# Context of batch 0 loaded in the front part of self-attention, its rounding released by the last residual

## The reference

```
x = layernorm(x + self_attention(x))          # 16 heads of 32, causal
x = layernorm(x + cross_attention(x, ctx))    # one head of 512: softmax(q k^T) v
x = layernorm(x + ffn(x))                     # a gated recurrence over the 16 batches
```

## Time and profile before

| | us |
|---|---|
| median of 3 runs | 1415.57 |
| lowest, highest | 1415.21, 1418.94 |
| the profiled execution | 1416.02 |
| its span | 1414.1 |
| self-attention, about | 0 to 381 |
| cross-attention, about | 381 to 837 |

### The profile page before, as it was taken

How to read it: one execution, slowest core, us unless ns; L and a number is a source line. 1 busy time by engine, 2 the same in 40 slices (tenths; PEclk the granted TensorE clock), 3 DMA queues, 4 the chain that set the end, 5 groups by cost and what they waited for, 6 DMA issues and landing times.

```text
span 1414.1 us, 28483 instructions
## 1 busy us (share of the span) xinstructions
PE 1385.4 (98%) x10017; PEld 1211.0 (86%) x10017; DVE 921.9 (65%) x1911; ACT 731.6 (52%) x1989; POOL 569.7 (40%) x475
## 2 busy tenths in 40 slices
PE   7999999999999999999999999999999999999997
PEld 4677777777789999999999988999999999999775
DVE  4589989999657756776677663345453444536697
ACT  4488888888565566656665655222232222222232
POOL 2476767676476565656565620000000000010264
PEclk9999999999999999999999999999999999999999
DMA  7014323335366675667567953010010100000353
GB/s 212 25 56 107 104 75 81 104 104 156 109 172 215 200 240 182 204 195 233 188 205 213 210 155 112 1 27 13 13 26 0 26 13 19 31 1 31 101 186 123
DMA packets 133079, 157.94 MB, mean 112 GB/s; under 512 B 62304, under 2 KB 70496, under 8 KB 133008
## 3 DMA queue, kind: packets, MB, share of 16 engines
q1 hardware_dynamic: 133008, 157.01, 37.8%
HBM read 105.61 MB, written 35.78 MB: 100 GB/s over the span
## 4 chain that ended last, share of the span: by engine, by line
PE 64%; issue 3%; POOL 3%; DMA 1%; DVE 1%; ACT 1%; POOLq 0%; ACTq 0%; DVEq 0%
PE banks L1522 16%; PE banks L1551 11%; PE banks L1007 9%; PE banks L1023 8%; PE banks L1036 6%; PE banks L1553 6%; PE banks L992 5%; POOL o_r L2097 1%; PE banks L977 1%; DMA s_cx_raw<-in_cx 1%; PE banks L1983 1%; PE banks L1053 1%; POOL o_rstd L2105 1%; POOL x_cx_lo L1367 1%; PE banks L2014 0%
## 5 line engine op out<-in xcount | busy, mean ns | idle before, releaser
L461 ACT ACTIVATE s_p<-banks,a_nmax 112x224 f32<-112x224 f32 (+1 forms) x512 | 198.1, 412 | 60.0 <-DVE a_nmax L572 59.9
L759 POOL TENSOR_TENSOR s_p<-s_p,a_rinv 112x896 f32<-112x896 f32 (+1 forms) x128 | 164.5, 1306 | 118.9 <-DVE a_rinv L580 115.8
L1496 POOL CAST m_hi<-w_raw 128x2048 fp32r<-128x2048 f32 x1 | 2.3, 2266 | 407.8 <-PE banks L1522 407.8
L1639 ACT ACTIVATE f_gate<-f_gate 128x448 f32<-128x448 f32 x90 | 52.2, 580 | 198.6 <-DVE f_gate L1762 198.6
L1759 DVE TENSOR_TENSOR f_gate<-banks,f_xg_early 128x448 f32<-128x448 f32 x45 | 28.1, 624 | 189.6 <-PE banks L1553 189.6
L1367 POOL TENSOR_TENSOR x_cx_lo<-s_cx_raw,x_cx_hi 125x512 fp32r<-125x512 f32 x96 | 120.8, 1296 | 37.0 <-ACT x_cx_hi L1136 37.0
L571 DVE TENSOR_REDUCE a_nmax<-banks 112x1 f32<-112x224 f32 x256 | 97.9, 382 | 24.5 <-PE banks L277 23.7
L461 ACT ACTIVATION_READ_ACCUMULATOR s_p<-banks,a_nmax 112x1 f32 x512 | 111.6, 218 | 0.0
L294 PEld LDWEIGHTS banks<-identity,s_p 112*112 112x112 f32 x768 | 88.0, 134 | 21.8 <-issue 2.3
L294 PE MATMUL banks<-identity,s_p 112*112 112x112 f32 x768 | 105.4, 261 | 1.2 <-POOL s_p L759 0.7
L1360 POOL TENSOR_TENSOR s_ct<-s_ct_raw,s_ct 128x750 fp32r<-128x750 f32 x60 | 98.6, 1669 | 0.0
(11 more groups left out here) (255 smaller groups left out, 3727.5 us busy)
## 6 DMA issues: line engine op xcount, KB each, us to landing
s_ct_raw<-in_ct SPq DMA_DIRECT2D x16, 1500.0 KB, 6.7
s_cx_raw<-in_cx SPq DMA_DIRECT2D x16, 1500.0 KB
a_xt<-in_xt SPq DMA_DIRECT2D x16, 448.0 KB, 6.3
a_xrow<-in_x SPq DMA_DIRECT2D x16, 448.0 KB, 5.9
a_xres<-in_x SPq DMA_DIRECT2D x16, 448.0 KB, 6.7
x_scratch<-a_xn SPq DMA_DIRECT2D x16, 448.0 KB, 3.3
x_scratch<-x_xn SPq DMA_DIRECT2D x16, 448.0 KB, 4.6
x_halves<-x_halves SPq DMA_DIRECT2D x16, 448.0 KB, 3.2
```

What stands on the lines that cost most here:

```text
L461: e = act.activation((p1 if c else p0)[:, g, h, :], src, ACT.Exp, bias=nmax[:, g % 2, c, h:h + 1], accum_out=rsum[:, g % 2, c, h:h + 1])
L759: pool.tensor_tensor(p[:, g, :, :], p[:, g, :, :], inv, ALU.mult).then_inc(norm_done, 1)
```

## The change

Two edits. In SP's program of self-attention the loads of ct and cx of batch 0 stand ahead of the loop over batches 4 to 13 instead of behind batch 14. On ScalarE the wait ahead of cross-attention's first step is for the last residual of self-attention (`r_done`) instead of its last norm (`xn_done`), and the wait for the last norm stands inside `exp` of batch 0.

```diff
@@ sync of self-attention
                 sp.dma_start(opening.c0[:], io["in_c"].rearrange("(k p) -> p k", p=128)).then_inc(opening.b_in, 16)
+            sp.dma_start(shared.ct_raw[:], io["ct"][0].rearrange("(k p) t -> p k t", p=128)).then_inc(shared.ct_in, 16)
+            sp.dma_start(shared.cx_raw[:], io["cx"][0].rearrange("(c p) d -> p c d", p=XR)).then_inc(shared.cx_in, 16)
             with sp.Fori(2, B // 2 - 1) as i:
                 for odd in range(2):
                     step(2 * i + odd, odd)
             step(B - 2, B % 2)
-            sp.dma_start(shared.ct_raw[:], io["ct"][0].rearrange("(k p) t -> p k t", p=128)).then_inc(shared.ct_in, 16)
-            sp.dma_start(shared.cx_raw[:], io["cx"][0].rearrange("(c p) d -> p c d", p=XR)).then_inc(shared.cx_in, 16)
             sp.wait_ge(stored, 16 * (B - 5))
@@ scalar of cross-attention
             def exp(b):
+                if isinstance(b, int) and b == 0:
+                    act.wait_ge(shared.xn_done, TC * B)
                 wait(act, pt_done, XC // 2 * b)
...
             x1th(1)
-            act.wait_ge(shared.xn_done, TC * B)
+            act.wait_ge(shared.r_done, TC * B)
             for b in range(2):
                 step(b)
```

## The result

The changed kernel took 1429.01 us (median; 1428.31 to 1430.27), the kernel before 1415.39 beside it: 1.0092 times the time, with a 95% interval of 1.0074 to 1.011. The profiled execution took 1429.4 us with a span of 1427.4, so it is 13.3 us of span above the one of before (1414.1). The forecast was 1428.0. Two single executions of later kernels lie far from all others of theirs and are left out of the ratios: 1485.17 us of the eighth (mean granted clock 0.885 instead of 0.995) and 2740.48 us of the twelfth (clock 1.0, cause unknown).

What follows compares the result with a forecast made beforehand. TensorE, busy 98% of the span, was taken to bound the kernel. The terms 12.9 (hold) + 1.5 (clock) - 2.0 (seam) + 0 (rounding) gave +12.4 us, so 1428.0 us, range 1420.4 to 1434.4.

Steps and rivals of the forecast that it cites:

- When xt lands: Early self-attention: batch 5's columns, queued behind ct and cx, land at 134.8 instead of 116.2 us; bounds 129.7 to 137.7.
- the x1 load that stood behind the same pair: At the old load place, x1 landed 26.0 us after ct's issue; the starting row for xt's landing.
- the 1.1 and 1.5 us taken off: From xt's landing estimate: 1.1 for a row load no longer ahead, 1.5 for two transfers instead of four pressing on engines.
- few engines: In xt's queue: cx's 125 partitions use 5 of 16 DMA engines, share 0.33 at 128 GB/s, and xt cannot pass.
- How long TensorE is held: At batch 4, TensorE waits through GpSimd for xt, going on at 139.5 instead of 126.6: 12.9 us, bounds 7.8 to 15.8.
- The clock: After TensorE's hold at batch 4, half clock costs 1.5 us, bounds 0 to 3.0.
- The six microseconds of the other row: Early part, 47 to 53 us: TensorE at clock 0.50 for six microseconds; half lost, giving the clock's upper bound 3.0.
- The seam: Between self- and cross-attention, loads gone, the store lands earlier and TensorE's 1.99 us wait shrinks: gain 2.0, bounds 0 to 3.0.
- The rounding: Start of cross-attention: ScalarE's earlier rounding of cx serves nobody, as GpSimd waits for the last norm: 0 us, at most 3.24.
- B: Rival at batch 4: xt passes cx on free engines, no hold, only the seam counts: 1413.6 us, chance 0.11.
- C: Rival at batch 4: both loads run at 391 GB/s, xt lands at 123.7, TensorE held 1.7 us: 1415.3 us, chance 0.06.
- D: Rival in cross-attention: earlier rounding advances the next cx load, removing TensorE's 2.07 us wait, on top of B: 1411.5, chance 0.04.

Runs made afterwards that it cites:

- eighth: Changed kernel with both loads issued behind batch 5's columns and batch 3's residual rows, cx split as 112 + 13 partitions: 1414.88 us, 0.9993.
- twelfth: Kernel before with ct ahead of the loop, rounding and GpSimd released by the last residual, subtractions before bias, next cx load before x1 rows: 1412.29 us, 0.9972.
- third: Changed kernel with only ct ahead of the loop, cx left behind batch 14: 1414.49 us, 0.9983.
- fourth: Changed kernel with only cx ahead of the loop, ct left behind batch 14: 1424.92 us, 1.0058.
- sixth kernel: Changed kernel with the front load of cx issued as two transfers, 112 + 13 partitions: 1422.44 us, 1.0046.
- second: Kernel before with only the earlier release of the rounding, loads at their old place: 1415.83 us, 0.999.
- tenth: Kernel before with only GpSimd's cross-attention released by the last residual, rounding still behind the last norm: 1415.41 us, 0.9993.
- first: Changed kernel with the rounding's earlier release undone, both loads still ahead of the loop: 1429.52 us, 1.0088.
- fifth: Changed kernel with ct and three of cx's six chunks ahead of the loop, the other three behind batch 14: 1421.68 us, 1.0043.
- ninth kernel: Kernel before with both the rounding and GpSimd's cross-attention released by the last residual, loads at their old place: 1420.51 us, 1.0031.

## Why the prediction was right

The sum was +12.4 us, measured +13.6, and for the reasons given:

- **When xt lands.** Forecast 134.8, measured 135.5. The working from the x1 load that stood behind the same pair held as a whole; the 1.1 and 1.5 us taken off were not tested singly. With cx alone in front the landing took 18.0 us where the row taken as the bound said 16.3. That cx is what delays xt is shown by the third and fourth kernels: 0 against 9.9 us for the same bytes. But the reason given, few engines, covers only a part: with both loads in front and all engines busy (sixth kernel) 8.60 of the 15.86 us of hold stay. The forecast had no term for that; it was inside the number because the row that it starts from had both loads in front, and to that extent the number is better than the reasoning.
- **How long TensorE is held.** Forecast 12.9, measured 13.3, through the waits named in the prediction: second pass of unit 16 (15.47 us, forecast "about 15"), split, first pass for unit 17, transposes at 139.92 (forecast 139.5).
- **The clock.** Forecast 1.5, measured 2.5, inside the bounds of 0 to 3.0. This is the term of the sum that was off most: I took the three microseconds at 0.50 behind an idle of 1.99 us, and it was over five after 139.9. The six microseconds of the other row would have been nearer; by them the term is 3.0. The length of the idle stretch doesn't give it either: behind unit 17's transposes the half clock lasted 5.3 us here (longest idle 10.73), about 4.0 behind cx alone (5.30) and about 6.2 in the sixth kernel (3.11), and the idle of 2.07 us at 422.67 in before was followed by none.
- **The seam.** Forecast 2.0, measured 2.24. TensorE's wait is 0.45 us (forecast about 0.5) and the clock stays at 1.00 from 374 to 384. A new wait of 0.92 us came at 385.5; the 2.24 are net of it. The second and tenth kernels, with before's loads and a clock that held, have it too (0.93 and 0.92), before, whose clock fell, has not; this fits what the prediction said, that VectorE's work comes due just after. That the clock falls at this place in only two of the four profiles with before's loads, and that half of the gain hangs on it, the forecast didn't see.
- **The rounding.** Forecast 0; the first and second kernels show 0 within what can be measured (1429.52 against 1429.01; 0.999).
- **The rivals.** B (xt passes cx) and C (full pace) fell with the landing of 22.4 us. C's pace is real for ct: 408 GB/s at share 1.02 with ct in front. The rule of the Trainium skill (DMA: Bandwidth & Descriptors, Bandwidth, "Measured") that transfers of 1 MiB or more reach 75% of a peak of 435 GB/s thus agrees with ct and not with cx, which had 125 to 128 GB/s; that table is for 128 partitions, which cx hasn't; its section "Why a DMA increments its semaphore by 16 and not by 1", which gives 125 partitions 5 of 16 engines, agrees with the 0.33 that before, after and the kernel with cx alone in front show. D's condition, that GpSimd waits for the rounding, is false in the kernels before and after, and true once GpSimd is released earlier (1.49 us, tenth kernel). But making it true by GpSimd's release alone brought no earlier load, and with the early rounding on top a loss of 4 us; only the twelfth kernel, which also changed the order on GpSimd and SP, got the load out earlier. The 2.07 us themselves are no measure of it: they are 0.34 in the first kernel, 1.20 in the tenth and gone in the third, fifth and eighth, with the load at 14.2 to 14.3 us after the store as ever, because TensorE had waited elsewhere and came there later.

## What to carry to other kernels

Before a large load is moved into a full stretch, look up its DMA share, not its bytes only: a copy that keeps only a few engines busy (here 125 partitions, a share of 0.33) takes long, and the small transfers issued behind it pay for that (xt 22.4 us instead of 4.5). Here it took both remedies to lose the hold, the load behind what is needed soon and split as 112 + 13 (hold 0.02); the split alone left 8.60 us, the later place alone 2.65. Then follow each transfer that now stands behind it to its waiting engine; what was made early at one place (7.3 us for xt with ct in front) may be made late at another (the store, 12.4 us). And an operation released earlier brings nothing until its consumer's own release and its place in the consumer's order are changed too.

## What the runs showed of the hardware that I had not expected

- **An issue can block SP for microseconds.** xt's issue lasted 9.07 us behind ct and cx, 5.41 behind cx, 3.38 behind ct and half of cx, 0.42 behind ct and the split cx, 0.39 behind ct. The issue next in SP's program is late with it (the residual rows at 122.49 instead of 112.69); the store at 127.18, which waits for VectorE, was not. What the issue waits for no view shows.
- **GpSimd can shut out VectorE.** The norm's two operations of 0.54 us took 9.85 us beside bias and subtractions without a pause, 2.76 with a pause of 1.49 us, and 2.62 beside subtractions alone, where the first of the two went on when the first subtraction ended. The first of the two took 8.45 us of the 9.85: it sat through the bias and five of the six subtractions. The Trainium skill (SBUF — State Buffer, "SBUF: two separate sides") says that VectorE and GpSimd lock a pair of ports against each other for a whole instruction, the loser waiting; on VectorE's side this is so for operations in a 2-port mode or with two inputs in SBUF. The row product `s_dot` has two such inputs; in which mode the norm runs the trace doesn't show. The 2.62 and 2.76 us agree: one GpSimd operation at most is waited for each time. The 8.45 us don't follow from it: a wait of one instruction would have ended at 383.2. Why VectorE got no turn between those subtractions, and did between the same ones in the twelfth kernel, stays open. It is no single case: `s_dot` took 0.69 us with GpSimd idle beside it (ninth kernel), 2.83 in before, 4.55 in the changed kernel and 9.24 in the eighth, each time beside GpSimd's bias and subtractions.
- **A full DMA share can hide little traffic.** Shares of 1.05 to 1.15 came with 141 to 316 GB/s from 118 to 126 us in the sixth kernel, with ct (until 120.0), the split cx, xt and residual rows under way, and 1.02 with 408 GB/s while ct and xt were under way in the third.
